# One-hots of the nodes split over three engines, a sum of squares moved to VectorE and the edge products put in another order, in a two-layer graph network kernel

## What is computed

```python
h = relu(layernorm(x));  x = x + adj_norm @ (h @ weight) + bias        # layer 0
h = relu(layernorm(x))                                                 # layer 1
s, v = (xs @ w_in2f_s)[idx_j], (xv @ w_in2f_v)[idx_j]                  # rows gathered to edges
W = (ssp(f_ij @ W1 + b1) @ W2 + b2) * rcut_ij                          # filters of the edges
edge = [s*ys*W0, sum_c(v*yv)*W1, s*yv*W2, v*ys*W3, ...]                # products
agg = segment_sum(edge, idx_i);  x = x + head(agg)
```

## Time and profile before

| what | us |
|---|---|
| median of 3 runs (lowest, highest) | 76.25 (75.9, 76.38) |
| the profiled execution, its own time | 75.25 |
| its span in the profile | 73.2 |

### The profile page before, as it was taken

How to read it: one execution, slowest core, us unless ns; L and a number is a source line. 1 busy time by engine, 2 the same in 40 slices (tenths; PEclk the granted TensorE clock), 3 DMA queues, 4 the chain that set the end, 5 groups by cost and what they waited for, 6 DMA issues and landing times.

```text
span 73.2 us, 1207 instructions
## 1 busy us (share of the span) xinstructions
PE 62.1 (85%) x407; PEld 48.6 (66%) x407; DVE 63.3 (86%) x141; ACT 46.3 (63%) x73; POOL 30.9 (42%) x41
## 2 busy tenths in 40 slices
PE   3996998999999998869986999995999988499530
PEld 1254664768442686849965899994999877397420
DVE  4699999999991999998899999999999999972670
ACT  0700089739996969762779858499959594732700
POOL 4000000003877100460337998967996957700000
PEclk9999999999999999999999999999999999999999
DMA  0899999973000000000000000000000000000035
GB/s 7 146 374 241 371 454 447 431 202 99 0 0 0 0 0 0 0 4 0 0 0 0 0 0 9 0 4 0 0 0 0 9 0 0 0 0 0 0 125 162
DMA packets 3049, 5.65 MB, mean 77 GB/s; under 512 B 540, under 2 KB 1936, under 8 KB 2916
## 3 DMA queue, kind: packets, MB, share of 16 engines
q1 hardware_dynamic: 2274, 5.14, 20.9%
q10 hardware_dynamic: 770, 0.44, 2.2%
HBM read 5.06 MB, written 0.52 MB: 76 GB/s over the span
## 4 chain that ended last, share of the span: by engine, by line
DVE 36%; PE 25%; ACT 14%; issue 10%; POOL 5%; DMA 3%; POOLq 2%; DVEq 0%; ACTq 0%
PE pair L711 13%; PE pair L694 6%; DVE W_all L394 4%; DVE Os L394 4%; ACT Mh L296 3%; DMA idx_sb<-idx 3%; POOL Ml L377 2%; PE pair L586 2%; DVE za L428 2%; PE pair L578 2%; DVE x L467 2%; DVE pair L503 2%; ACT OsR L233 2%; DVE hW_lo L458 2%; DVE hX L431 2%
## 5 line engine op out<-in xcount | busy, mean ns | idle before, releaser
L711 PE MATMUL pair<-OsR,Mh 128*128 128x256 f32 x68 | 17.5, 294 | 3.0 <-POOL Ml L377 1.7
L711 PE MATMUL pair<-OsR,Ml 128*128 128x256 f32 x68 | 16.7, 281 | 0.0
L711 PEld LDWEIGHTS pair<-OsR,Mh 128*128 128x128 f32 x68 | 12.8, 188 | 4.5 <-ACT OsR L233 2.8
L711 PEld LDWEIGHTS pair<-OsR,Ml 128*128 128x128 f32 x68 | 12.8, 188 | 0.0
L377 POOL TENSOR_TENSOR Ml<-dst_bc,Mh 128x512 fp32r<-128x512 f32 x8 | 10.4, 1304 | 4.7 <-ACT Mh L296 4.7
L694 PE MATMUL pair<-HL,OdT 128*128 128x256 f32 x68 | 9.7, 284 | 1.1 <-DVE HL L492 0.8
L694 PEld LDWEIGHTS pair<-HL,OdT 128*128 128x128 f32 x68 | 8.7, 188 | 1.4 <-DVE OdT L441 1.0
L578 PE MATMUL pair<-W_all,Os 128*128 128x256 bf16 x68 | 8.7, 282 | 0.8 <-DVE W_all L394 0.7
L578 PEld LDWEIGHTS pair<-W_all,Os 128*128 128x128 bf16 x68 | 6.6, 100 | 4.2 <-DVE W_all L394 2.3
L381 POOL TENSOR_TENSOR Ml<-dst_bc,Mh 128x512 fp32r<-128x512 f32 x7 | 9.1, 1306 | 0.0
L233 ACT ACTIVATE OsR<-Os 128x1024 fp32r<-128x1024 bf16 (+1 forms) x9 | 8.9, 1001 | 0.0
(11 more groups left out here) (117 smaller groups left out, 130.8 us busy)
## 6 DMA issues: line engine op xcount, KB each, us to landing
dst_bc<-dst_row SPq DMA_DIRECT2D x1, 2176.0 KB, 13.5
w_sb<-w SPq DMA_DIRECT2D x1, 1024.0 KB, 8.4
x_sb<-x SPq DMA_DIRECT2D x1, 512.0 KB, 4.7
out<-x_sb SPq DMA_DIRECT2D x2, 192.0 KB, 1.9
f_sb<-f_t SPq DMA_DIRECT2D x1, 378.0 KB
b_sb<-bias SPq DMA_DIRECT2D x1, 256.0 KB, 13.7
w_sb<-w ACTq DMA_DIRECT2D x1, 128.0 KB, 4.4
out<-x_sb ACTq DMA_DIRECT2D x1, 128.0 KB, 1.9
```

Of the source, the lines that this page charges most:

```text
L711: last = nc.tensor.matmul(bank[4 + b][:, 0:N], part[:, g % RG, j, feats(b)], OsR[:, g % RG, j, :], start=(t == 0 and part is Mh), stop=(t ...
```

## The change

The node one-hots `OdT` are split anew: ACT makes a = 1, first half; DVE makes a = 0, first half, in two pieces of 1088 edges; POOL makes the second half of both, behind DVE's pieces. The second sum of squares goes from ACT to DVE. DVE's `hY` moves behind the wait for `scales`, and its three `scaled_filters` move behind `Hl` and the second piece. On POOL the scaling of `o1s` moves ahead, and `scaled_late(g)` moves into the loop. The products of a group stand in another order, with the one of svw ahead of the reduction in the last two groups only.

```diff
@@ ACT
-            nc.scalar.activation(gap[:], dst_bc[:, E // 2:], ACT.Abs, bias=iota_n[:, 1:2]).then_inc(q["gap"], 1)
+            nc.scalar.activation(gap[:], dst_bc[:, 0:E // 2], ACT.Abs, bias=iota_n[:, 1:2]).then_inc(q["gap"], 1)
...
-            nc.scalar.activation(OdT[:, 1, E // 2:], gap[:], ACT.Relu, bias=one[:, 0:1], scale=-1.0).then_inc(q["OdTa"], 1)
+            nc.scalar.activation(OdT[:, 1, 0:E // 2], gap[:], ACT.Relu, bias=one[:, 0:1], scale=-1.0).then_inc(q["OdTa"], 1)
...
-            for a in range(NH):
-                act.wait_ge(q[("neg_h2", "h2")[a]], 1)
...
+            act.wait_ge(q["neg_h2"], 1)
+            nc.scalar.activation(za[:, 0:D], h2[:, 0, :], ACT.Square, accum_out=sq[:, 0:1]).then_inc(q["sq0"], 1)
@@ POOL
+            pool.wait_ge(q["sq0"], 1)
+            pool.wait_ge(q["sq1"], 1)
...
+            pool.wait_ge(q["OdT"], 2)
+            for a in range(NH):
+                nc.gpsimd.tensor_scalar(OdT[:, a, E // 2:], dst_bc[:, E // 2:], iota_c[:, a:a + 1], None,
+                                        ALU.is_equal).then_inc(q["OdTp"], 1)
...
-            scaled_late(3)
-            scaled_late(4)
...
-                if g + 5 < NG:
-                    scaled_late(g + 5)
+                if g + PRE < NG:
+                    scaled_late(g + PRE)
@@ DVE
-            dve.wait_ge(q["hhi"], 2)
-            nc.vector.tensor_tensor(hY[0:64, :], za[64:128, :], hY[64:128, :].bitcast(fp32), ALU.subtract).then_inc(q["hYlo"], 1)
...
             dve.wait_ge(q["scales"], 1)
+            dve.wait_ge(q["hhi"], 2)
+            nc.vector.tensor_tensor(hY[0:64, :], za[64:128, :], hY[64:128, :].bitcast(fp32), ALU.subtract).then_inc(q["hYlo"], 1)
...
-            node_onehots(0, 0)
+            nc.vector.scalar_tensor_tensor(xb[:, 1, :], h2[:, 1, :], 1.0, h2[:, 1, :], ALU.mult, ALU.mult,
+                                           accum_out=sq[:, 1:2]).then_inc(q["sq1"], 1)
...
-            scaled_filters(0)
-            scaled_filters(1)
-            node_onehots(1, 0)
+            first_onehots(0, E // 4)
...
-            node_onehots(0, 1)
+            first_onehots(E // 4, E // 2)
+            scaled_filters(0)
+            scaled_filters(1)
             scaled_filters(2)
...
                 if g == 2:
-                    dve.wait_ge(q["OdT"], 3)
+                    dve.wait_ge(q["OdTp"], 2)
@@ PE, gather
                 if g == 0:
-                    pe.wait_ge(q["OdT"], 2)
+                    pe.wait_ge(q["OdT"], 1)
+                    pe.wait_ge(q["OdTa"], 1)
...
                 if (TG * g + tiles(g)) * P > E // 2:
-                    pe.wait_ge(q["OdT"], 3)
-                    pe.wait_ge(q["OdTa"], 1)
+                    pe.wait_ge(q["OdTp"], 2)
```

More of the change, by code:

```diff
@@ L145, in gnn_preln_kernel @@
                  "onehot adj CI CT A degve scales hW_hi hW_lo L0 xb x1 "
-                 "h2 neg_h2 tp2 h2T0 h2T sq ve2 s2 H Hh Hl "
+                 "h2 neg_h2 tp2 h2T0 h2T sq0 sq1 ve2 s2 H Hh Hl "
                  "z zabs zexp zln hT hhi hXlo hYlo w2hi w2lo ones b2r b2p W Wsb "
-                 "y WY WYp negc gap OdTa OdT OsR "
+                 "y WY WYp negc gap OdTa OdTp OdT OsR "
                  "G Glo add m0 vys sw2 vyv svw red MA MhA MhB MlA MlB MlA_late MlB_late scat "
@@ L251, in _ @@
                                  scale=-float(D)).then_inc(q["neg_h2"], 1)
-            for a in range(NH):
-                act.wait_ge(q[("neg_h2", "h2")[a]], 1)
[L255 to L260, removed]
+            act.wait_ge(q["neg_h2"], 1)
+            nc.scalar.activation(za[:, 0:D], h2[:, 0, :], ACT.Square, accum_out=sq[:, 0:1]).then_inc(q["sq0"], 1)
+            act.wait_ge(q["tp2"], 1)
+            nc.scalar.activation(h2T[:, 0, :, :], bank[6][:, :], ACT.Relu, scale=-1.0).then_inc(q["h2T0"], 1)
             def filters_out(g):
@@ L513, in _ @@
                 m = M[:, o, 0:n, :].rearrange("p t (k f) -> p t k f", k=S)
+                if g == 0:
+                    dve.wait_ge(q["OdT"], 2)
                 if g == 2:
-                    dve.wait_ge(q["OdT"], 3)
+                    dve.wait_ge(q["OdTp"], 2)
                 dve.wait_ge(q["add"], g + 1)
@@ L522, in _, with times_y @@
                     dve.wait_ge(q["MlA"], g - RG + 1)
[L523 removed]
+                def times_y():
+                    dve.wait_ge(q["sw2"], g + 1)
+                    nc.vector.tensor_tensor(m[:, :, 2:8:2, :], G[:, :, 0:1, :].broadcast_to((P, n, 3, F)), yv,
+                                            ALU.mult).then_inc(q["svw"], 1)
                 nc.vector.tensor_tensor(m[:, :, 3:8:2, :], v, wy[:, :, 1:2, :].broadcast_to((P, n, 3, F)),
                                         ALU.mult).then_inc(q["vys"], 1)
+                nc.vector.tensor_tensor(m[:, :, 0, :], sn, wy[:, :, 0, :], ALU.mult).then_inc(q["m0"], 1)
+                dve.wait_ge(q["vys"], g + 1)
+                nc.vector.tensor_tensor(v, v, yv, ALU.mult).then_inc(q["vyv"], 1)
                 dve.wait_ge(q["m0"], g + 1)
                 nc.vector.tensor_tensor(sn, sn, w[:, :, 0, :], ALU.mult).then_inc(q["sw2"], 1)
[L528 to L529 removed]
+                if g + 2 >= NG:
+                    times_y()
                 dve.wait_ge(q["vyv"], g + 1)
@@ L532, in _ @@
                                         ALU.add).then_inc(q["red"], 1)
-                dve.wait_ge(q["sw2"], g + 1)
-                nc.vector.tensor_tensor(m[:, :, 2:8:2, :], G[:, :, 0:1, :].broadcast_to((P, n, 3, F)), yv,
-                                        ALU.mult).then_inc(q["svw"], 1)
+                if g + 2 < NG:
+                    times_y()
                 dve.wait_ge(q["red"], g + 1)
```

22 lines of the change are left out of this document (11 added, 11 removed).

## The result

| what | us |
|---|---|
| kernel after, median of 4 runs (lowest, highest) | 82.33 (81.7, 82.97) |
| kernel before, beside it, median of 4 runs | 76.08 (75.31, 76.38) |
| ratio, 95% interval | 1.084 (1.071 to 1.096) |
| profiled execution of after: its time, its span | 81.7, 79.9 |
| the forecast and its range | 77.1, 75.9 to 79.0 |

The change makes the kernel 8% slower: the side forecast, but far outside the range. The four times lie in two pairs, 81.70 and 81.75, 82.90 and 82.97 us, and the profiled execution is one of the first pair. The page of after answers to the earlier trace rows; under it stands the row of the granted clock in forty slices of 2 us, which was 9 throughout before.

The account below looks back on a forecast made before the run. The prediction took the loop to be bound by a ring through all four engines, entered at svw(0). Its sum, +1.05 (first gather) - 0.12 (products) - 0.08 (end) = +0.85 on 76.25, gave 77.1 us, range 75.9 to 79.0.

Parts of the forecast that it names:

- Layer 0: With hY behind the first scales, A and the scales come some 0.9 us earlier; gain 0, at most 0.1.
- Square and first gather: Square on DVE worth little; filters(2) waits for scaled filters behind Hl and the second piece, making group 0's row sum 1.05 late.
- The products: New order saves 0.12 us ahead of the reduction in groups 0 to 6; the ring keeps only that ahead of svw(0).
- POOL's one-hots: Two of 2176 elements on POOL, taken at 2.2 us each, done before POOL's next duty; cost 0.
- Each us over 3.3 costs 2: Beyond 3.3 us per POOL one-hot, without cover, each further us costs 2 us, as there are two.
- the cover: POOL's 6.7 us from the second piece's end at 33.2 to MlB(0) at 39.9, in which its one-hots cost nothing.
- long one-hots: Rival: POOL's one-hots outlast their cover; at 4.2 us each 78.7, at 5.6 us 81.5; chance 0.17.
- the mark of being right: Sign: PE idle over 1 us before filters(2), released by DVE's W_all.
- DVE is the bound all along: Rival, not slower: each group keeps its 0.12 us, early svw saves 0.2 more, 1.05 is gone: 76.3; chance 0.21.
- hY behind POOL: Rival: in layer 0 POOL's second scale holds DVE's hY, +0.35 to +0.85 us more, 77.45 to 77.95; chance 0.20.

Follow-up runs that it names:

- before_filled: The kernel before with three spare matmuls of zeros on PE ahead of gather(0): 75.28 us, ratio 0.998.
- skipped_filled: The kernel after without POOL's two one-hots (second-half gathers read the first half's), with eight spare PE matmuls ahead of filters(2): 76.06 us, ratio 1.007.
- after_filled: The kernel after with spare PE matmuls of zeros, eight ahead of filters(2) and 18 ahead of scatter(0): 80.69 us, ratio 1.068.
- order_only: The kernel before with only the new order of a group's products: 75.91 us, ratio 0.998.
- pool_prices: The kernel before with six unused POOL instructions (one-hots, a multiplication, copies) at the end of the edge loop: 79.42 us in one execution.

## Why the prediction was wrong, step by step

The runs give a sum that the forecast can be laid beside, all medians, and all but the last at full clock: `before_filled` 75.28; + 0.78 for everything but POOL's one-hots and the clock (`skipped_filled` 76.06); + 4.63 for POOL's one-hots (`after_filled` 80.69); + 1.64 for the half clock (after, 82.33; 1.0 or 2.2 in single executions, as above). It rests on runs with one thing changed at a time, two of which leave out half of the one-hots.

- *Layer 0.* Right: hW_lo(1) starts at 24.56 behind ACT, and x1 at 26.53, 0.05 earlier than in before.
- *Square and first gather.* Right: filters(2) was forecast for 33.56 and came at 33.36, the row sum of group 0 at 36.03 and came at 35.92 where PE had its full clock. Of the 0.20 us at filters(2), 0.12 is that Hl(1) starts at 31.93 and not 32.05; the steps behind it took what the forecast gave them (0.26, 0.69), and the last 0.08 lies between the scaled filters and PE. In after itself the row sum is at 37.26, by the half clock.
- *The products.* Right: in after the reduction starts 0.20 behind its small neighbour (39.19, then 39.39 us) and gives way in 0.46; `order_only` shows no gain that can be told, as the 0.2 of the sum would have it. Together with the first gather the forecast's +0.85 stands beside +0.78.
- *POOL's one-hots.* This is the step that failed: "I take 2.2, near the IOTA, since one tensor is read". It measured 5.79, over the 5.6 that the text had as its upper end. The rule beside it was right. "Each us over 3.3 costs 2" gives 2 x (5.79 - 3.3) = 5.0 us, and 4.63 was measured; the cover ended at 39.9 in the forecast, and without POOL's one-hots the first subtraction starts at 39.79. What was wrong was to choose between ends so far apart by an argument, that the number of inputs sets the price. `pool_prices` speaks against it: all six of its instructions read one tensor, and the four that compute cost 2.5 times the two that only copy or cast. The row L358, the only one of the same operation, was put aside as held by DVE. That reading was right, as the same instruction took 0.29 in after, where DVE left it alone, but it left the price unknown, and the chance of 0.17 for long one-hots was too small for that. At 5.6 us that rival had 81.5 (its own rule, 2 x 2.3 on top of 77.1, gives 81.7), where 80.69 came without the half clock and 82.33 with it. That looks closer than it is: the forecast stands on 76.25, a median that lies in the upper heap; on 75.28, without it, the same sum is 80.7.
- *The half clock.* Missing altogether. The forecast saw that PE would be idle for over 1 us ahead of filters(2), named it as the mark of being right, and gave the wait no price beyond its length; a second wait, ahead of scatter(0), came with POOL's one-hots. Behind the two the half clock costs 1.0 us in the profiled execution and 1.6 by the medians. The Trainium skill, TensorE: Matmul & The Clock Gate, section "What's actually happening", has the rule that an idle TensorE falls back to half its clock and is released by work; the windows of after agree, 0.50 behind both waits.
- *The rivals.* "DVE is the bound all along" falls by `order_only`. "hY behind POOL" falls by the row of hY: 22.21, at its forecast time and 1.35 long. It went the other way: POOL's y took 1.04 instead of 0.41 and ended 0.28 behind hY, without anyone waiting for it.

## What to carry to other kernels

Before work is given to an engine that is off the critical path, measure its price there at the size in question, and write down when that engine is next wanted: up to that point the work is free (one one-hot of 5.8 us cost nothing here), beyond it each microsecond cost nearly a microsecond (4.9 us late, 4.63 longer), however idle the engine looked over the whole span. Price a new wait of TensorE by what the clock does behind it as well as by its length; where one can't be removed, spare matmuls in the gap gave the clock back (1.0 to 2.2 us here). And read single times for heaps: a median that falls between two heaps 1 us apart moves with the share of each, and differences of half a microsecond can be told only heap by heap, or once what parts them is removed.

## What the runs showed of the hardware that was not expected

- On GpSimd a TENSOR_SCALAR takes 1.50 to 1.59 us for 128x512, 2.84 for 128x1024 and 5.79 for 128x2176, about what a subtraction of two tensors takes (1.3 for 128x512), whatever the operation, the types or the kind of scalar; COPY and CAST take 0.61 for 128x512. Small ones mislead: the scaling of 32x128 took 0.29 and one of 128x2 0.19, which looks like 0.8 ns an element, where 512 to 1024 elements give 2.4.
- TensorE's granted clock was at 0.50 behind waits of 1.88, 3.14, 3.63 and 7.08 us, and behind 0.8 us ahead of gather(0) in about half of the executions, for the next 2.7 to 5.3 us of work. It was at 1.00 behind a wait of 1.63 us that stood behind 18 spare matmuls; matmuls of zeros were enough for that.
- Beside a one-hot of 2.84 us on GpSimd, a VectorE instruction with two inputs from SBUF, 128x256 and 0.42 us otherwise, took longer but was not held to the end. VectorE in `pool_prices`:

```profile
70.39 0.87 DVE L570 TENSOR_TENSOR za<-za 128x256 f32<-128x256 f32 x1
```

It ended at 71.26, while the one-hot ran from 69.87 to 72.71. By the Trainium skill, SBUF — State Buffer, section "Who interferes with whom", it would have waited for the whole of it; this row disagrees. Another row agrees with the rule: POOL's y, which started beside hY, ended 0.28 behind it. What makes the two cases differ is not settled by these runs.
